# The first stretch of a token mixer, written out straight, with its rows made two chunks ahead

## The chip, the core and the metric

The kernel runs on one core of one Trainium2 chip. The metric is device time in microseconds (us), the median of several runs. The engines are TensorE (PE in the rows; PEld is its weight load), VectorE (DVE), ScalarE (ACT), GpSimd (POOL) and SyncE (SP), which here only issues DMAs.

## What is computed

```python
xn = layernorm(x)                                 # x: (4, 1024, 256), eps 1e-5, no scale or shift
out = x + attention(xn) + experts(xn)
# attention: q, k, v = xn @ W + b, 16 heads of 16, causal softmax, @ Wo + bo
# experts:   scores = softmax(xn @ gate_w.T), top 4 of 16, weights normalised
#            y = sum_e w_e * (silu(xn @ w_gate[e]) * (xn @ w_up[e])) @ w_down[e]   (width 176)
#            + a shared expert of width 352, kept as two tiles of 176
```

All is float32. The kernel keeps float32 operands as pairs of float16, a high and a low half, and multiplies high by high, high by low and low by high.

## The kernel before

The program has three blocks, between which all engines meet: `prepare`, `route`, `attention_and_experts`. The change is in `prepare` alone.

`prepare` walks through the 4096 tokens in 8 chunks of 512 rows (NCH = 8), each 4 tiles of 128 (TPC = 4). For every chunk:

- GpSimd issues the load of X (two buffers). VectorE takes the statistics (`variances`: bn_stats, bn_aggr, L445 adds eps, L447 the reciprocal), ScalarE takes the square root (`root`, L353), VectorE refines it by a Newton step of four chained four-element instructions (`newton`, L452 to L455) and normalises (`normalise`, L459, into XN).
- ScalarE makes the high half of the rows (`rows_high`, L360), VectorE the low half (`rows_low`, L465), TensorE turns both (`turn`, L540), ScalarE copies them out (`columns`, L370, into XT).
- TensorE makes q and k in four products (L554, two PSUM buffers), ScalarE copies each out twice (`product`, L386 in float32, L389 as high half), VectorE makes the low half (`low_half`, L469). Then come the router's logits (L565) and the values (L575; copied by VectorE, `values`, L477).
- Two experts' weights are split: ScalarE the high halves (`weights_high`, L377 and L378), VectorE the low halves (`weights_low`, L487 and L490). Float32 weights are staged in two buffers (gu_stage and dn_stage). GpSimd issues the three loads of an expert (`load_expert`, L281 to L283) when the low half of the tile that used the buffer before is made (semaphore `lo_made`).
- SP stores rows, columns, q, k and values to DRAM.

Each engine has its own queue of instructions, written out by hand in a function `step(c, p, first, last)`, and waits on semaphores. In step c the engines make q, k, v and logits of chunk c and the rows of chunk c + 1. ScalarE's order in a step is product 0, product 1, root and rows_high of c + 1, first expert, product 2, product 3, columns of c + 1, logits, second expert. VectorE's is variances of c + 1, low halves 0 and 1, normalise and rows_low of c + 1, first expert, low halves 2 and 3, values, second expert. `over_steps` writes steps 0, 1, 6 and 7 out and runs steps 2 to 5 as a loop of two iterations of two steps. The two shared tiles are split before step 0, experts 2c and 2c + 1 in step c.

Ahead of the steps GpSimd issues the loads of X for chunks 0 and 1 and of the two shared tiles, then fills V, woP, Vs and Ks (L301 to L305, Ks with ONES in one instruction of 6144 elements a partition) and makes identity and mask tiles (L313, L322).

Of the kernel before, what the change touches and what calls it, by code (L numbers as in the profile page):

```python
# [10 lines left out]
ALU = mybir.AluOpType  # L11
ACT = mybir.ActivationFunctionType
AX = mybir.AxisListType
P = 128
# [110 lines left out]
def wait_apart(eng, sem, value, passed):  # L125

    eng.wait_ge(sem, value)
    eng.sem_inc(passed, 1)


# [19 lines left out]
def prepare(nc, s):  # L150
# [6 lines left out]
    EPC = E // NCH  # L157
    assert EPC == SH == 2 and NCH % 2 == 0 and NCH >= 6 and s.QC == 2 and s.HG == 2 * MO
    with ExitStack() as ctx:
# [8 lines left out]
        gu = sb("gu_stage", [P, EPC, HC, 2, I])  # L168
        dn = sb("dn_stage", [IP, EPC, 2, D])
# [10 lines left out]
        rfin = sb("rfin", [P, TPC])  # L180
        F = sb("F", [P, 2, CH])
# [9 lines left out]
        sp_passed = sem("sp_passed"); dve_passed = sem("dve_passed")  # L191
        const_set = sem("const_set"); const_made = sem("const_made"); wo_clear = sem("wo_clear"); wo_in = sem("wo_in")
        gu_in = [sem(f"gu_in{i}") for i in range(EPC)]; hi_made = sem("hi_made"); lo_made = sem("lo_made")
# [4 lines left out]
        rstd_done = sem("rstd_done"); nw_done = sem("nw_done"); xn_done = sem("xn_done"); xhi = sem("xhi"); xlo = sem("xlo")  # L198
# [3 lines left out]
        xr_st = sem("xr_st"); xt_st = sem("xt_st"); qk_st = [sem(f"qk_st{i}") for i in range(4)]; v_st = sem("v_st")  # L202
# [5 lines left out]
        def over_steps(eng, step):  # L208


            for p in range(2):
                step(p, p, True, False)
            with eng.Fori(1, NCH // 2 - 1) as cc:
                for p in range(2):
                    step(cc * 2 + p, p, False, False)
            for p in range(2):
                step(NCH - 2 + p, p, False, True)

        def more(p, last):

            return not (last and p == 1)

        @block.sync
        def _(sp):
# [17 lines left out]
            def store_rows(c, p):  # L242
                wait_apart(sp, xlo, TPC * (c + 1), sp_passed)
                sp.dma_start(s.xrow_d[bass.ds(c * CH, CH), :].rearrange("(j p) d -> p j d", p=P),
                             XR[:, p].rearrange("p j a d -> p j (a d)")).then_inc(xr_st, 16)

            def step(c, p, first, last):
                wait_apart(sp, xt_done, TPC * (c + 1), sp_passed)
                sp.dma_start(s.xcol_d[bass.ds(c * TPC, TPC)].rearrange("j p f -> p j f"),
                             XT[:, p].rearrange("p j a c t -> p j (a c t)")).then_inc(xt_st, 16)  # L250
                for i in range(4):
                    dst, m = (s.q_d, s.k_d)[i // MO], i % MO
                    b = c // 2 if isinstance(c, int) else (c - p) // 2
                    wait_apart(sp, f2_done, 4 * c + i + 1, sp_passed)
                    sp.dma_start(dst[bass.ds(b, 1), :, 2 * m:2 * m + 2, :, :, :, p * CH:(p + 1) * CH]
                                 .rearrange("o a g e r j t -> (o g e r j) a t"), F2[:, i]).then_inc(qk_st[i], 16)
                    if i == 0 and more(p, last):
                        store_rows(c + 1, 1 - p)
                wait_apart(sp, v_out, 2 * HG * (c + 1), sp_passed)
                b = c // 2 if isinstance(c, int) else (c - p) // 2  # L260
                w = TPC * s.VW
                sp.dma_start(s.v_d[bass.ds(b, 1), :, :, p * w:(p + 1) * w].rearrange("o g p x -> p (o g) x"),
                             V[:, :, :].rearrange("p (g x) e -> p g (x e)", g=HG)).then_inc(v_st, 16)

            store_rows(0, 0)
            over_steps(sp, step)
            sp.wait_ge(wo_in, 16 * (4 * HG + 1))
            sp.wait_ge(xr_st, 16 * NCH)
            sp.wait_ge(xt_st, 16 * NCH)
# [5 lines left out]
        def _(pool):  # L275
            def load_x(p, src):
                pool.dma_start(X[:, p], src.rearrange("(j p) d -> p j d", p=P)).then_inc(x_in[p], 16)

            def load_expert(n, g, u, d):

                pool.dma_start(gu[:, n, :, 0, :], g.rearrange("(c p) i -> p c i", p=P)).then_inc(gu_in[n], 16)  # L281
# [3 lines left out]
            for p in range(2):  # L285
                load_x(p, s.xf[p * CH:(p + 1) * CH, :])
# [11 lines left out]
            for n in range(SH):  # L298
                c = slice(n * I, (n + 1) * I)
                load_expert(n, s.sw_gate[:, c], s.sw_up[:, c], s.sw_down[c, :])  # L300
# [4 lines left out]
            pool.memset(s.Ks[:, :, :, :], ONES).then_inc(k_ones, 1)  # L305
            pool.wait_ge(k_ones, 1)
# [17 lines left out]
            pool.wait_ge(const_made, 2)  # L324

            def step(c, p, first, last):
                if not last:

                    pool.wait_ge(xn_done, TPC * (c + 1))
                    load_x(p, s.xf[bass.ds((c + 2) * CH, CH), :])  # L330
                for n in range(EPC):
                    e = c * EPC + n
                    pool.wait_ge(lo_made, 2 * (c * EPC + n + 1))
                    load_expert(n, *(w[bass.ds(e, 1)].rearrange("o r c -> (o r) c") for w in (s.w_gate, s.w_up, s.w_down)))
# [1222 lines left out]
```

## Time and profile before

| | us |
|---|---|
| median of 3 runs | 1351.32 |
| lowest, highest | 1346.31, 1351.62 |
| the profiled execution, whole | 1356.54 |
| its span | 1354.9 |
| `prepare` in it | 0 to 142.4 |
| `route` | 142.4 to 168.9 |
| `attention_and_experts` | from 168.9 |

Over the whole span the profile has TensorE busy for 1007.9 us (74%), VectorE for 866.0 (64%), ScalarE for 654.5 (48%) and GpSimd for 579.2 (43%). All times below are us from the start of the span. An instruction's row gives its start and its duration; in brackets stand the idle time of its engine before it and what ended that. For a DMA the duration is that of its issue; the time to landing stands in the DMA view. PEclk is the share of TensorE's full clock that was granted.

### The profile page before, as it was taken

The numbers are of one execution on the slowest core, as the hardware profiler recorded it, in microseconds if no ns is written. First come the engines' busy times: TensorE is split into PE (matmuls) and PEld (weight loads), VectorE is DVE, ScalarE is ACT, GpSimd is POOL, SyncE is SP. The second block draws the span as 40 slices with busy tenths as digits, with TensorE's granted clock in tenths as the row PEclk, the third lists the DMA queues.
The fourth block names the chain that finished last, engine by engine and source line by source line (L and its number), as shares of the span: only waits on it lengthen the run. The fifth ranks groups of instructions, "written<-read, shape, count | busy, mean of one in ns | idle before, by whom it ended". The sixth has DMA issues, their size and how long they took to land.

```text
span 1354.9 us, 26394 instructions
## 1 busy us (share of the span) xinstructions
PE 1007.9 (74%) x8634; PEld 525.7 (39%) x8634; DVE 866.0 (64%) x1784; ACT 654.5 (48%) x1219; POOL 579.2 (43%) x531
## 2 busy tenths in 40 slices
PE   2788121010399999898998989998988989899885
PEld 1555010000144444444544444454444445444433
DVE  6888831000288887777777676676767676677553
ACT  3778100000154545565566666556666665566341
POOL 6333177776200000454366666435656553464100
PEclk9888555555599999899999999999989999899888
DMA  6899450010113131443545355354535353444702
GB/s 175 270 297 283 125 180 1 1 34 1 43 56 105 54 104 48 88 85 75 89 80 112 63 111 95 66 89 78 111 57 112 56 112 64 88 71 73 134 17 31
DMA packets 99484, 126.41 MB, mean 93 GB/s; under 512 B 24873, under 2 KB 83514, under 8 KB 98834
## 3 DMA queue, kind: packets, MB, share of 16 engines
q0 software_dynamic: 41632, 60.79, 25.0%
q1 hardware_dynamic: 57730, 63.99, 16.1%
q8 instruction: 77, 1.26, 0.4%
q14 instruction: 45, 0.37, 0.1%
HBM read 71.63 MB, written 57.80 MB: 96 GB/s over the span
## 4 chain that ended last, share of the span: by engine, by line
PE 53%; DVE 10%; another core or an unknown queue 10%; issue 9%; ACT 2%; SPq 1%; DMA 1%; POOL 0%; ACTq 0%; DVEq 0%
PE gup L1221 12%; PE pvp L1144 10%; PE outs L1248 9%; DVE part L1314 6%; PE smp L1100 6%; PE turn L1233 4%; PE stp L1125 4%; PE outs L1151 3%; PE turn L1191 3%; PE smp L1083 1%; ACT probs L1484 1%; DVE hf L1371 1%; DVE sg L1366 1%; DMA Qs<-nm 1%
## 5 line engine op out<-in xcount | busy, mean ns | idle before, releaser
L1484 ACT ACTIVATE probs<-stp 128x1024 f32<-128x1024 f32 (+1 forms) x320 | 300.4, 939 | 424.4 <-remote 205.2
L1314 DVE TENSOR_REDUCE part<-smp 128x2 f32<-128x256 f32 (+2 forms) x372 | 345.9, 951 | 140.0 <-remote 72.5
L942 POOL DMA_INDIRECT XG<-xrow_d,slots x144 | 146.8, 1019 | 247.0 <-DMA out<-Y 201.7
L1221 PE MATMUL gup<-gu_w,XC 128*128 (+1 forms) x1152 | 212.8, 321 | 32.7 <-issue 21.8
L1100 PE MATMUL smp<-Ks,Qs 48*128 48x128 f16 (+2 forms) x744 | 112.5, 341 | 103.7 <-DVE part L1314 52.4
L1248 PE MATMUL outs<-dn_w,h 88*128 (+1 forms) x1248 | 183.6, 280 | 0.1
L949 POOL DMA_INDIRECT out<-Y,slots x72 | 117.1, 1626 | 139.1 <-ACT Y L1517 107.8
L1144 PE MATMUL pvp<-probs,Vs 128*32 128x512 f32 (+3 forms) x1536 | 168.8, 512 | 0.8 <-DVE probs L1413 0.7
L949 POOL DMA_INDIRECT acc_d<-Y,slots x72 | 114.7, 1594 | 123.7 <-ACT Y L1517 104.6
L1221 PEld LDWEIGHTS gup<-gu_w,XC 128*128 128x128 f16 x1152 | 107.2, 99 | 96.1 <-issue 43.5
L931 POOL DMA_INDIRECT slot_d<-entry,slot_i x128 | 124.3, 971 | 41.6 <-issue 41.6
L1366 DVE SCALAR_TENSOR_TENSOR sg<-th,gup 128x176 f32<-128x176 f32 x208 | 69.8, 336 | 106.6 <-ACT th L1490 69.3
L1376 DVE TENSOR_TENSOR h<-turn,h 88x256 f16<-88x256 f32 x208 | 86.6, 416 | 78.1 <-ACT h L1496 67.2
L1248 PEld LDWEIGHTS outs<-dn_w,h 88*128 88x128 f16 x1248 | 123.3, 99 | 29.3 <-issue 2.5
L1496 ACT ACTIVATE h<-turn 88x256 f16<-88x256 f32 x208 | 78.3, 377 | 115.5 <-PE turn L1233 110.5
L1125 PE MATMUL stp<-Qs,Ks 50*128 50x512 f16 (+3 forms) x768 | 118.7, 332 | 16.2 <-DMA Qs<-nm 8.0
L1100 PEld LDWEIGHTS smp<-Ks,Qs 48*128 48x128 f16 x744 | 28.9, 94 | 199.8 <-DVE part L1314 99.8
L1233 PE MATMUL turn<-ident,hf 128*88 128x128 f32 x416 | 87.7, 294 | 22.9 <-issue 17.8
L1413 DVE TENSOR_TENSOR probs<-probs,keepk 128x512 f32<-128x512 f32 x128 | 87.7, 685 | 22.9 <-ACT probs L1484 16.3
L1490 ACT ACTIVATE th<-gup 128x176 f32<-128x176 f32 x208 | 66.4, 319 | 53.8 <-PE gup L1221 35.2
L1501 ACT ACTIVATE XC<-turn 128x512 f16<-128x512 f16 x144 | 85.3, 593 | 5.3 <-PE turn L1191 4.0
L1517 ACT ACTIVATE Y<-outs,slots 128x256 f32<-128x256 f32 x144 | 68.0, 472 | 31.9 <-PE outs L1248 27.9
(170 smaller groups left out, 1109.6 us busy)
## 6 DMA issues: line engine op xcount, KB each, us to landing
rb<-rsum_d SPq DMA_DIRECT2D x60, 128.0 KB
Ks<-k_d SPq DMA_DIRECT2D x96, 64.0 KB
Qs<-q_d SPq DMA_DIRECT2D x96, 64.0 KB
v_d<-V SPq DMA_DIRECT2D x8, 544.0 KB, 4.6
Vs<-v_d SPq DMA_DIRECT2D x16, 272.0 KB, 3.0
acc_d<-YA SPq DMA_DIRECT2D x1, 4224.0 KB
X<-L_attn_x POOLq DMA_DIRECT2D x8, 512.0 KB, 5.0
xrow_d<-XR SPq DMA_DIRECT2D x8, 512.0 KB, 5.0
```

Of the source, the lines that this page charges most:

```text
L931: pool.indirect_dma_start(s.slot_d, bass.IndirectOffsetOnAxis(ap=s.slot_i[:, i:i + 1], axis=0), s.entry[:, i, :], None).then_inc(scattered ...
L942: pool.indirect_dma_start(XG[:, q].rearrange("p a c t -> p (a c t)"), None, s.xrow_d, bass.IndirectOffsetOnAxis(ap=slots[:, r, 0:1], axis= ...
L949: pool.indirect_dma_start((s.out, s.acc_d)[r % 2], bass.IndirectOffsetOnAxis(ap=slots[:, r, 0:1], axis=0), Y[:, r % YB], None, compute_op= ...
L1100: last = pe.matmul(banks[:, e, col:col + w], Qs[rows, buf, j, t * P:(t + 1) * P], Ks[rows, buf, j, k0:k0 + w], start=i == 0, stop=k0 + w < ...
L1125: last = pe.matmul(stp[:, e, i * w:(i + 1) * w], Ks[rows, buf, j, t * P:(t + 1) * P], Qs[rows, buf, j, q * CH + q0:(q + 1) * CH], start=i ...
L1144: last = pe.matmul(pvp[32 * h:32 * h + 32, q0:CH], Vs[:, buf, o:o + 2 * DK], probs[:, st % PB, h * w:(h + 1) * w], start=t == 0, stop=t == ...
L1221: last = pe.matmul(gup[:, 0:2 * I], columns[:, a, h], weights_of(s.gu_w, e, b, h, slice(0, 2 * I)), start=n == 0, stop=n == 5)
L1233: last = pe.transpose(hp[:, c * P:(c + 1) * P], hf[:, v % FB, c * IP:(c + 1) * IP], s.ident[:, :])
L1248: last = pe.matmul(yp, h16[:, v % 2, a, c], weights_of(s.dn_w, e, b, c, slice(0, D)), start=begin and n == 0, stop=end and n == 5)
L1314: last = dve.tensor_reduce(part[:, g % 2, k0 // CH, :, j, t], banks[:, :, col:col + w], AX.X, ALU.max)
L1413: dve.tensor_tensor(block, block, s.keepk[:, :].rearrange("p (h k) -> p h k", h=1).broadcast_to([P, 4, P]), ALU.min).then_inc(masked, 1)
L1484: act.activation(to, of, ACT.Exp, scale=float(DK) ** -0.5 / QS ** 2).then_inc(exp_done, 1)
```

## The change

- `over_steps`, its loop and `wait_apart` go: all 8 steps are written out, with constant indices.
- The rows are made two chunks ahead: chunks 0 and 1 ahead of step 0, chunk 2 in step 0, chunk c + 2 in step c; the statistics of chunk c + 3 at the end of step c. The transposes and `columns` stay one chunk ahead. `rows_high` and `rows_low` of c + 2 come behind the second pair of products (step 0 has an order of its own).
- The Newton step goes from VectorE to GpSimd, ahead of the step's loads there.
- Both (or three) weight tiles of a step stand at its end, on ScalarE and VectorE. Step 0 has the two shared tiles, steps 1 to 5 have experts 0 to 9, step 6 has 10, 11 and 12, step 7 has 13, 14 and 15. The two stage buffers stay.
- Ks is filled by six instructions of 1024 elements a partition, in steps 0, 1, 6 and 7 of GpSimd's queue, instead of one ahead of the steps.
- TensorE turns chunk 0 before the gate's weights, and waits for the gate's low half only ahead of the first logits. Semaphores of the row and column stores are doubled.

The core of the diff (a short rename of indices is left out):

```diff
+        SPLITS = [[E, E + 1]] + [[2 * c - 2, 2 * c - 1] for c in range(1, NCH - 2)] + [[10, 11, 12], [13, 14, 15]]
+        ORDER = [e for step in SPLITS for e in step]
...
 @block.sync
+            def step(c):
...
+                if later(c, 2) is not None:
+                    store_rows(c + 2)
+                sp.wait_ge(v_out, 2 * HG * (c + 1))
...
 @block.gpsimd
+            def load_expert(k):
+                e, n = ORDER[k], k % 2
+                if k >= 2:
+                    pool.wait_ge(lo_made, 2 * (k - 1))
...
+            def newton(c):
+                def then(i, ins):
+                    ins.then_inc(nw_done, 1)
+                    pool.wait_ge(nw_done, 3 * c + i + 1)
+                pool.wait_ge(rstd_done, c + 1)
+                then(0, pool.tensor_tensor(nw[:, 0], rstd[:, :], rstd[:, :], ALU.mult))
+                then(1, pool.tensor_tensor(nw[:, 1], nw[:, 0], re_[:, :], ALU.mult))
+                then(2, pool.tensor_scalar(nw[:, 2], nw[:, 1], -0.5 / (XS * XS), 1.5, ALU.mult, ALU.add))
+                if c:
+                    pool.wait_ge(xn_done, TPC * c)
+                pool.tensor_tensor(rfin[:, :], rstd[:, :], nw[:, 2], ALU.mult).then_inc(rfin_done, 1)
...
+            newton(0)
             pool.memset(V[:, :, DK:DK + 1], 1.0).then_inc(v_ones, 1)
...
-            pool.memset(s.Ks[:, :, :, :], ONES).then_inc(k_ones, 1)
...
+            load_x(2)
+            newton(1)
+            load_x(3)
+            newton(2)
+
+            def step(c):
+                if later(c, 2) is not None and c:
+                    newton(c + 2)
+                if c < 2 or c >= NCH - 2:
+                    for b in range(c % 2, NB, 2):
+                        pool.memset(s.Ks[:, b, 0 if c < 2 else 1], ONES).then_inc(k_ones, 1)
+                if c:
+                    first = sum(len(x) for x in SPLITS[:c])
+                    for k in range(first, first + len(SPLITS[c])):
+                        load_expert(k)
+                if c + 4 < NCH:
+                    load_x(c + 4)
...
 @block.scalar
+            def step(c):
                 product(c, 0)
+                if c and later(c, 2) is not None:
+                    root(c + 2)
                 product(c, 1)
-                if more(p, last):
-                    root(c + 1)
-                    rows_high(c + 1, 1 - p)
-                weights_high(c, 0)
+                if c == 0:
+                    rows_high(1)
+                    act.wait_ge(gt_out, 1)
+                    act.activation(g16[:, 0], gT32[:, :, :], ACT.Copy, scale=WS).then_inc(w_hi, 1)
                 product(c, 2)
                 product(c, 3)
-                if more(p, last):
-                    columns(c + 1, 1 - p)
+                if c == 0:
+                    root(2)
+                elif later(c, 2) is not None:
+                    rows_high(c + 2)
                 act.wait_ge(lg_done, c + 1)
...
+                if later(c, 1) is not None:
+                    columns(c + 1)
+                if c == 0:
+                    rows_high(2)
+                first = sum(len(x) for x in SPLITS[:c])
+                for k in range(first, first + len(SPLITS[c])):
+                    weights_high(k)
...
 @block.vector
+            def step(c):
                 low_half(c, 0)
                 low_half(c, 1)
+                if c and later(c, 2) is not None:
+                    normalise(c + 2)
+                if c == 0:
+                    rows_low(1)
+                    variances(2)
+                    dve.wait_ge(w_hi, 4)
+                    dve.scalar_tensor_tensor(out=g16[:, 1], in0=gT32[:, :, :], scalar=WS, in1=g16[:, 0],
+                                             op0=ALU.mult, op1=ALU.subtract).then_inc(w_lo, 1)
                 low_half(c, 2)
                 low_half(c, 3)
+                if c == 0:
+                    normalise(2)
+                elif later(c, 2) is not None:
+                    rows_low(c + 2)
                 values(c, 0)
                 values(c, 1)
+                if c == 0:
+                    rows_low(2)
+                if later(c, 3) is not None:
+                    variances(c + 3)
+                first = sum(len(x) for x in SPLITS[:c])
+                for k in range(first, first + len(SPLITS[c])):
+                    weights_low(k)
+
+            variances(0)
+            normalise(0)
+            variances(1)
+            rows_low(0)
...
 @block.tensor
+            pe.wait_ge(const_made, 1)
+            turn(0)
             pe.wait_ge(b_in, 16 * (2 * HG + 2))
...
+            pe.wait_ge(w_lo, 3)
+            for c in range(NCH):
+                step(c)
```

`later(c, n)` is c + n, or None where there is no such chunk.

## Rows read from the trace of the kernel before

**Rows 1.** Busy time by stretch: PE, PEld, DVE, ACT, POOL, then PEclk, DMA share, GB/s
```profile
69.87:85.59 15.72, 12.44 (x98) 7.89 (x97) 12.80 (x38) 11.95 (x24) 5.11 (x7) 0.78 0.96 306
85.59:100.10 14.51, 11.28 (x98) 6.92 (x96) 12.76 (x38) 9.82 (x21) 5.11 (x7) 0.88 0.86 264
...
114.37:128.24 13.87, 11.06 (x98) 7.04 (x97) 12.51 (x38) 10.84 (x24) 4.44 (x7) 0.88 0.89 272
128.24:142.40 14.16, 8.95 (x81) 5.24 (x80) 9.66 (x22) 8.70 (x16) 2.18 (x3) 0.90 0.89 295
...
168.90:360.00 191.10, 21.03 (x155) 8.81 (x155) 24.52 (x31) 1.34 (x2) 134.01 (x142) 0.50 0.16 44
```

**Rows 2.** TensorE in order of time: the first products of chunks 0, 1, 7
```profile
25.60 7.84 PE L554 MATMUL qk<-XT,w 128*128 128x512 f16 x24 [1.39 <-ACT XT L370]
...
41.37 5.58 PE L554 MATMUL qk<-XT,w 128*128 128x512 f16 x24
...
128.24 5.59 PE L554 MATMUL qk<-XT,w 128*128 128x512 f16 x24
```

**Rows 3.** Waits until 143 us: total, number, longest
```profile
PE tp L540 <- DVE XR L465: 25.9, 8, 6.6
```

**Rows 4.** ScalarE in order of time: copies of a product, high halves of experts
```profile
66.52 0.67 ACT L386 ACTIVATE F<-qk,bqk 128x512 f32<-128x512 f32 x1
67.09 0.68 ACT L389 ACTIVATE F<-qk,bqk 128x512 f16<-128x512 f32 x1
...
78.58 0.78 ACT L377 ACTIVATE gu_w<-gu_stage 128x704 f32 x1
79.26 0.62 ACT L378 ACTIVATE dn_w<-dn_stage 88x512 f32 x1
...
138.27 0.79 ACT L377 ACTIVATE gu_w<-gu_stage 128x704 f16<-128x704 f32 x1 [2.35 <-DMA dn_stage<-L_ffn_w_down]
```

**Rows 5.** VectorE in order of time: ahead of chunk 0, and the refining of chunk 3
```profile
10.02 5.85 DVE L445 TENSOR_SCALAR re_<-mv 128x4 f32<-128x4 f32 x1
...
17.54 1.65 DVE L459 TENSOR_SCALAR XN<-X,mv,rfin 128x256 f32<-128x256 f32 x4
...
19.21 1.28 DVE L514 TENSOR_TENSOR w<-F,w 128x512 f16<-128x512 f32 x2
...
21.84 1.43 DVE L465 TENSOR_TENSOR XR<-XN,XR 128x256 f16<-128x256 f32 x4 [0.56 <-ACT XR L360]
...
28.98 1.39 DVE L438 BATCH_NORM_STATS2 st<-X 128x6 f32<-128x256 f32 x4
...
30.73 0.17 DVE L445 TENSOR_SCALAR re_<-mv 128x4 f32<-128x4 f32 x1
...
61.50 0.15 DVE L452 TENSOR_TENSOR nw<-rstd 128x4 f32<-128x4 f32 x1
...
62.09 0.16 DVE L455 TENSOR_TENSOR rfin<-rstd,nw 128x4 f32<-128x4 f32 x1
```

**Rows 6.** GpSimd in order of time: before the steps, and the first of an expert's issues
```profile
8.66 0.77 POOL L283 DMA_DIRECT2D dn_stage<-L_ffn_sw_down  x1
...
10.61 5.23 POOL L305 MEMSET Ks<- 128x6144 f16 x1
15.99 0.95 POOL L313 TENSOR_SCALAR_AFFINE_SELECT idh<-idh 64x256 bf16<-64x256 bf16 x2
...
67.44 0.71 POOL L281 DMA_DIRECT2D gu_stage<-L_ffn_w_gate  x1 [2.19 <-DVE dn_w L490]
```

**Rows 7.** DMA view, three stretches: GB/s by slice; issues, KB, median us to landing
```profile
GB/s 357 363 353 218 192 176 376 398 360 345 232 43 335 373 354 363 315 152 212 364 327 356 299 276 82 204 380 366 376 302 224 181 220 354 351 254 271 181 246 303
...
dn_stage<-L_ffn_w_down POOLq DMA_DIRECT2D x16, 176.0 KB, 5.6
...
dn_stage<-L_ffn_w_down POOLq DMA_DIRECT2D x2, 176.0 KB, 4.2
...
dn_stage<-L_ffn_sw_down POOLq DMA_DIRECT2D x2, 176.0 KB, 7.0
```

More of the change, by code:

```diff
@@ L206, in flat, with one, expert_parts, later @@
             return w.rearrange("p c n -> p (c n)")
[L208 to L221, printed above, removed]
+        def one(t):
+            return t.rearrange("p o c n -> p (o c) n")
+        def expert_parts(e):
+            e = slice(e, e + 1) if isinstance(e, int) else bass.ds(e, 1)
+            return ([one(s.gu_w[:, e, a]).rearrange("p c (a i) -> p c a i", a=2) for a in range(2)],
+                    [one(s.dn_w[:, e, a]) for a in range(2)])
+        SPLITS = [[E, E + 1]] + [[2 * c - 2, 2 * c - 1] for c in range(1, NCH - 2)] + [[10, 11, 12], [13, 14, 15]]
+        ORDER = [e for step in SPLITS for e in step]
+        assert sorted(ORDER) == list(range(E + SH))
+        def later(c, ahead):
+            return c + ahead if c + ahead < NCH else None
         @block.sync
@@ L297, in _ @@
             last.then_inc(const_made, 1)
[L298 to L300 removed]
+            for k in range(SH):
+                load_expert(k)
+            newton(0)
             pool.memset(V[:, :, DK:DK + 1], 1.0).then_inc(v_ones, 1)
@@ L324, in _ @@
             pool.wait_ge(const_made, 2)
[L326 to L334, printed above, removed]
-            over_steps(pool, step)
-            pool.wait_ge(k_ones, 1)
-        def one(t):
-            return t.rearrange("p o c n -> p (o c) n")
-        def expert_parts(c, n):
-            e = slice(E + n, E + n + 1) if c is None else bass.ds(c * EPC + n, 1)
-            return ([one(s.gu_w[:, e, a]).rearrange("p c (a i) -> p c a i", a=2) for a in range(2)],
-                    [one(s.dn_w[:, e, a]) for a in range(2)])
+            load_x(2)
[11 more added lines that the diff above has]
+                    for k in range(first, first + len(SPLITS[c])):
+                        load_expert(k)
+                if c + 4 < NCH:
+                    load_x(c + 4)
+            for c in range(NCH):
+                step(c)
+            pool.wait_ge(k_ones, 2 * NB)
         @block.scalar
@@ L557, in step @@
                     x.then_inc(qk_done, 1)
-                if more(p, last):
-                    turn(c + 1, 1 - p)
-                if began:
+                if later(c, 1) is not None:
+                    turn(c + 1)
+                if c:
                     pe.wait_ge(lg_out, c)
+                else:
+                    pe.wait_ge(w_lo, 4)
                 for j in range(TPC):
@@ L584, in _ @@
             last.then_inc(gt_done, 1)
-            turn(0, 0)
-            pe.wait_ge(w_lo, 4)
-            over_steps(pe, step)
+            pe.wait_ge(w_lo, 3)
+            for c in range(NCH):
+                step(c)
 def route(nc, s):
```

204 lines of the change are left out of this document (88 added, 116 removed).

## Prediction

> **What bounds the kernel now.** I read the stretch by stretch table first. The change touches only the first stretch, up to 142.40 us; behind it come routing and 191 us in which TensorE is nearly idle and GpSimd busy, then attention with the experts [rows 1]. All engines leave the first stretch together, so a microsecond won or lost before 142.40 moves everything behind it by as much, and nothing later gets shorter. Next, TensorE's timeline: chunk 0 begins at 25.60, chunk 1 at 41.37, chunk 7 at 128.24 [rows 2]. Chunks 1 to 6 take (128.24 - 41.37) / 6 = 14.5 us each; chunk 7 with the end of the stretch takes 14.2. In a chunk TensorE works some 11.1 us and else stands mostly at the transposes of the next rows, 25.9 us in eight waits [rows 1, 3]: these rows are normalised, split and turned within the chunk, VectorE and ScalarE in turns. VectorE works 12.5 to 12.8 us a chunk, ScalarE 9.8 to 12, and the DMA share is 0.86 to 0.96 [rows 1]. No compute in the middle waits for an expert's load: one whose three issues start at 67.44 is first read at 78.58; only the last expert is waited for, 2.35 us [rows 4, 6].
>
> **The start.** VectorE's four-element add at L445 takes 5.85 us in chunk 0 and 0.17 in chunk 1, and it ends as GpSimd's 5.23 us fill of Ks ends [rows 5, 6]. That fill is cut into six slices and spread. The add then ends near 10.2, the reciprocal at 10.4, the root at 10.6. The refining of the root is now GpSimd's, behind its first loads, the last of which is issued at 8.66 [rows 6]. Its price N no row shows. Lower bound: on VectorE the four chained steps take 0.8 us [rows 5]. Upper bound: two chained selects of GpSimd take 0.95, so four 1.9 [rows 6], and some 2.5 if VectorE's operations hold them up; the held add is no bound, since it was held by a fill of 6144 elements. I take N = 1.3, nearer to the lower row, as these have four elements a partition: 11.9. GpSimd then fills V, woP and Vs, 1.4 us, and normalising is of the kind that was held at L445: 13.3. Then VectorE in its new order: normalising 1.6, statistics of chunk 1 2.0, low halves of the rows 1.3, low halves of the weights 1.9, to 20.1 [rows 5]. TensorE turns and ScalarE copies chunk 0 beside it, so chunk 0 starts at 20.3 for 25.60. **Gain 5.3.** The gate's transposes hide behind chunk 0's turn.
>
> The Trainium skill (GPSIMD Engine Reference, Key points) says that GpSimd shares its SBUF interfaces with VectorE and that VectorE is about twice as fast for elementwise work. By it the refining would be some 1.6 us instead of 0.8, and each round of the loop below 0.3 longer. The held add of 5.85 us agrees with the sharing [rows 5].
>
> **Chunk 0.** From its start: rows of chunk 1 low at 8.4, then VectorE makes chunk 2's statistics (2.1) and the gate's low half (0.2), on which the logits now wait, 10.7; logits 0.9, values 3.3: 14.9, for 15.77 now. So chunk 1 starts at 35.2 for 41.37. By then VectorE is behind: values to 36.0, low rows of chunk 2 37.4, statistics of chunk 3 39.4, root 39.6, refining 40.9, a Ks slice (5.23 / 6 = 0.87) 41.8. Only now come the loads of step 1: five issues ahead of the last at 0.71 to 0.77 each (3.6 us), the last one's landing, and its high half. The landing is 5.6 us as the median of sixteen, 4.2 at the light end, 7.0 for six issues on end at the start [rows 6, 7]; I take 5.5. 41.8 + 3.6 + 5.5 + 1.2 = 52.1. I call this moment H(1): ScalarE done with step 1's second expert.
>
> **The loop that then sets the pace.** Before, an expert's load waits for its stage alone. Now the refining stands on GpSimd's queue ahead of six issues; its root stands on ScalarE behind product(c,0), and that behind the high halves of the step before. From H to H: product(c,0), two activations at a pitch of 0.57, 1.1; root and hand-over 0.3; N 1.3; five issues 3.6; landing 5.5; high halves of gu and dn 1.3 [rows 4, 6, 7]. **13.1 us.** VectorE's own work is 12.5 in a straight chunk less 0.8 of refining, 11.7; TensorE's 11.1 [rows 1, 5]. The traffic is 512 KB each for X, xrow and xcol, four times 256 for q and k, 544 for v and six times 176 for experts, 4.26 MB; at the 340 to 390 GB/s of the full slices it takes 10.9 to 12.5 [rows 7]. All lie under 13.1. So H(5) = 52.1 + 4 x 13.1 = 104.5: 1.4 us a chunk less than now.
>
> **The tail, where most of it goes back.** Steps 6 and 7 make three experts each, with two stages. The third load of a step waits for the low half of the step's first expert, which VectorE makes behind the step's values. Counted from H(5): qk of chunk 6 to 4.0, turn, logits and values on TensorE 5.4: 9.4, and chunk 7 may start, at 113.9, 14 us ahead of now. VectorE's values 10.3, low half of expert 10 11.7, expert 12's load 1.4 to its last issue and 5.2 to land, 18.3, high half 19.6 = H(6). ScalarE stands at it, and the products of chunk 7 are queued behind; TensorE makes two of them and idles some 8 us. Then two copies of products 22.0, the last qk 23.5, logits and values 27.3, VectorE 28.2, low half of expert 13 29.6, and only then expert 15's load: 1.4 + 5.0, 36.0; its high and low halves 38.1; all leave at 38.2. The stretch ends at 104.5 + 38.2 = **142.7** for 142.40. From where chunk 7 may start it is 28.8 us, for 14.2 now [rows 1, 4].
>
> **Edges at nothing.** Straight code: chunk 6, straight now, takes 13.9, those of the loop up to 15.7, so straight code isn't starved, and what it saves is off the loop above [rows 1]. SP's row store goes behind four product stores, and chunk 0's column store behind the rows of chunk 1; their readers come a chunk later, and what they cost is what is missing to that. X is loaded behind the experts and read 10 us later. The 17 loads of wo begin 3 us later on SP and are wanted at the end. The late Ks slices run while GpSimd waits for stages.
>
> **The sum.** The profiled execution is 1354.9 in span and 1356.54 in all, 5.2 over the median of 1351.32. The change is +0.3: 1356.8, or 1351.6 on the median. I say **1352**, since a schedule made by hand forgets waits oftener than it invents them.
>
> **Rivals.** *Forecast*, 1345 to 1358: start and pace gain 14 us and the tail gives them back. 0.62.
> *Loads land sooner.* With the light landing of 4.2 and N at 0.8 the loop is 11.3, and VectorE's 11.7 decides: H(5) = 50.3 + 46.8 = 97.1, the tail 2 shorter, the end 133.3: 9 us gained, 1342. For it: steps 6 and 7 load no X and store no rows. Against: 5.6 is the median now, and the same bytes will come closer together. If the tail moreover takes 14 us as now, 1337. Together 0.20. The Trainium skill (DMA: Bandwidth & Descriptors, Anatomy of one DMA) gives about 2.0 us and bytes over 436 GB/s for a GpSimd DMA, as an estimate 2.4 for 176 KB; the loop would be 10.0, and VectorE's 11.7 would decide as well. The rows of 4.2 to 7.0 speak against it under this traffic [rows 7].
> *The queue of loads takes the place of the wait removed: slower.* 4.26 MB in 13.1 us is 325 GB/s, for 264 to 306 now [rows 1]. With a landing of 6.5 and N 2.1 the loop is 14.9: H(5) = 53.9 + 59.6 = 113.5, the tail 2 longer, the end 153.7: 1362. Landing and N together decide: slower than before from 6.8 on (6.8 is what I take), by over 0.5% from about 8.1. For it: the 7.0 at the start; against: the issues alone take 4.4 us of each loop and leave the queue gaps. 0.18.
> *Rows two chunks ahead bring nothing*, since ScalarE's queue holds them: the time of the forecast, which has that in its loop.
>
> **Numbers.** A measurement can tell about 0.5%, 6.8 us. Faster 0.20, same 0.62, slower 0.18. The 80% range takes in most of both rivals, 1342 to 1360.
>
> **What would show it.** Right: L445's first instance at 0.2 us and the first product at 20 to 21; chunk starts 13 us apart from chunk 2 on; ScalarE waiting for dn_stage's landing in each step; TensorE idle for 8 us within chunk 7; a last expert load issued near 134, the routing's first reduction at 142 to 144. Wrong: chunks under 12 us apart or ScalarE never waiting for a load, a routing start before 137; or refining operations of over 0.6 us each, or landings over 6.5.

## The result, and the profile after

The changed kernel is slower: 1368.8 us as the median of six runs (1364.8 to 1372.5) against 1351.5 of the kernel before in the same six rounds (1346.3 to 1357.3), a ratio of 1.0123 with an interval of 1.0093 to 1.0154. Forecast was 1352, with a range up to 1360. The profiled execution took 1367.0 in span and 1368.74 in all, for 1354.9 and 1356.54 before. The first stretch now ends where routing's first reduction starts. Behind that point the two profiles are alike: 1354.9 - 142.5 = 1212.4 before, 1367.0 - 155.8 = 1211.2 after. The loss lies in the first stretch and is 13.3 us there.

```profile
155.81 0.69 DVE L723 TENSOR_REDUCE mx<-logits 128x32 f32<-128x512 f32 x1 [0.33 <-PEq L152]
```

TensorE in order of time, the pairs of products of the changed kernel, to be held against [rows 2]. "x12" is one pair; in brackets the idle time before it.

```profile
20.25 8.11 PE L579 MATMUL qk<-XT,w 128*128 128x512 f16 x24 [1.07 <-ACT XT L388]
36.16 2.75 PE L579 MATMUL qk<-XT,w 128*128 128x512 f16 x12
...
49.90 2.76 PE L579 MATMUL qk<-XT,w 128*128 128x512 f16 x12 [2.02 <-ACT XT L388]
57.86 5.30 PE L579 MATMUL qk<-XT,w 128*128 128x512 f16 x12 [5.20 <-ACT F L405]
67.80 2.76 PE L579 MATMUL qk<-XT,w 128*128 128x512 f16 x12 [0.27 <-ACT XT L388]
72.27 2.76 PE L579 MATMUL qk<-XT,w 128*128 128x512 f16 x12 [1.70 <-ACT F L405]
...
116.80 4.91 PE L579 MATMUL qk<-XT,w 128*128 128x512 f16 x12 [5.55 <-ACT F L405]
...
125.86 2.75 PE L579 MATMUL qk<-XT,w 128*128 128x512 f16 x12
137.10 5.00 PE L579 MATMUL qk<-XT,w 128*128 128x512 f16 x12 [8.48 <-ACT F L405]
```

The 5.4 us of the start are there: chunk 0 begins at 20.25 for 25.60, chunk 1 at 36.16 for 41.37. By chunk 7 most is gone, 125.86 for 128.24. From there the stretch takes 29.9 us for 14.3. The eight waits for the transposes' rows [rows 3] have become one, ahead of chunk 0; in the middle TensorE now waits for ScalarE to copy a product out ("ACT F").

The windows of the changed kernel, with the columns of [rows 1], are cut at the chunk starts:

```profile
36.16:49.90 13.74, 10.01 (x99) 6.14 (x96) 13.67 (x43) 10.61 (x22) 9.31 (x13) 1.00 0.81 255
49.90:67.80 17.90, 12.43 (x96) 6.93 (x97) 11.76 (x34) 10.88 (x23) 7.04 (x12) 0.81 0.92 271
67.80:79.70 11.90, 9.84 (x97) 6.20 (x97) 11.17 (x33) 10.52 (x22) 7.00 (x11) 1.00 0.93 298
79.70:96.20 16.50, 11.44 (x96) 6.62 (x97) 12.65 (x38) 10.88 (x23) 6.70 (x11) 0.90 0.96 299
...
125.86:155.70 29.84, 11.18 (x82) 5.87 (x79) 14.01 (x28) 12.06 (x21) 9.77 (x13) 0.71 0.53 163
```

Chunk 1 is filled by VectorE (13.67 of 13.74). Chunks 2 to 6 last about 12 and 17 us in turns, 15.2 on average, and no engine is busy for that long: in the three shown VectorE has 11.2 to 12.7, ScalarE 10.5 to 10.9. So a chain with waits sets the pace. The last window is the tail, where VectorE and ScalarE together have 26 us of work in 29.8, no more than if they worked in turns. The waits of the changed kernel up to 156 us (total, number, longest) name the links:

```profile
POOL nw L300 <- ACT rstd L372: 44.9, 8, 9.2
...
PE qk L579 <- ACT F L405: 29.5, 8, 8.5
ACT gu_w L394 <- DMA dn_stage<-L_ffn_w_down: 28.5, 10, 7.3
POOL gu_stage L289 <- DVE dn_w L506: 25.9, 5, 9.5
```

ScalarE waits for the landing of an expert's third load ten times, 28.5 us in all. Before it did so once, for 2.35 [rows 4]. GpSimd waits for the root eight times; in five of them, in steps 1 to 5, the step's loads are queued behind that wait. TensorE waits for ScalarE, which stands at the weights. That is a ring: root, refining, loads, landing, high halves, next root. One round of it, from GpSimd's and then ScalarE's timeline in step 1:

```profile
40.97 0.51 POOL L300 TENSOR_TENSOR nw<-rstd 128x4 f32<-128x4 f32 x1 [4.18 <-ACT rstd L372]
41.56 1.35 POOL L301 TENSOR_TENSOR nw<-nw,re_ 128x4 f32<-128x4 f32 x1
42.99 0.51 POOL L302 TENSOR_SCALAR nw<-nw 128x4 f32<-128x4 f32 x1
43.58 0.52 POOL L305 TENSOR_TENSOR rfin<-rstd,nw 128x4 f32<-128x4 f32 x1
...
48.62 0.77 POOL L291 DMA_DIRECT2D dn_stage<-L_ffn_w_down  x1
```

```profile
55.35 0.79 ACT L394 ACTIVATE gu_w<-gu_stage 128x704 f16<-128x704 f32 x1 [3.29 <-DMA dn_stage<-L_ffn_w_down]
56.04 0.61 ACT L395 ACTIVATE dn_w<-dn_stage 88x512 f16<-88x512 f32 x1
```

The four refining steps take 3.1 us here, from 40.97 to 44.10. The last load is issued at 48.62 and ScalarE's high half starts at 55.35, 6.7 us later. H(1), the moment at which ScalarE is done with step 1's second expert, is 56.6. The same reading gives H at 71.0, 86.0, 99.9 and 115.6 for steps 2 to 5, one round every 14.7 us. Below, H is always the start of the last L395 (or what that line has become) of a step plus 0.6.

### The profile page after: what moved, and what is told of

It reads as the page before. It is cut to its first block, busy times and chain, and to the rows that moved or that the text cites. A ratio compares the mean times of both kernels' runs of the same rounds, so it can differ in the third digit from the quotient of the medians.

```text
span 1367.0 us, 25847 instructions
## 1 busy us (share of the span) xinstructions
PE 1005.0 (74%) x8634; PEld 520.2 (38%) x8634; DVE 855.5 (63%) x1752; ACT 654.6 (48%) x1220; POOL 596.0 (44%) x568
## 3 DMA queue, kind: packets, MB, share of 16 engines
q1 hardware_dynamic: 57730, 63.99, 16.2%
## 4 chain that ended last, share of the span: by engine, by line
PE 49%; another core or an unknown queue 14%; DVE 9%; issue 8%; DMA 2%; SPq 2%; ACT 2%; POOL 0%; ACTq 0%; DVEq 0%
PE gup L1249 11%; PE pvp L1172 9%; PE outs L1276 8%; PE smp L1128 5%; DVE part L1342 5%; PE turn L1261 4%; PE stp L1153 4%; PE outs L1179 3%; PE turn L1219 2%; DMA Qs<-nm 1%; PE smp L1111 1%; ACT probs L1512 1%; DVE sg L1394 1%; DVE hf L1399 1%
## 5 line engine op out<-in xcount | busy, mean ns | idle before, releaser
L1276 PEld LDWEIGHTS outs<-dn_w,h 88*128 88x128 f16 x1248 | 122.6, 99 | 29.8 <-issue 4.0
```

What stands on the lines that cost most here:

```text
L1276: last = pe.matmul(yp, h16[:, v % 2, a, c], weights_of(s.dn_w, e, b, c, slice(0, D)), start=begin and n == 0, stop=end and n == 5)
```

## The experiments

**Three theories.** R: the ring sets the pace, and the refining's place ahead of the loads is what makes it. S: there are too few stages (two buffers for two or three experts), so that loads start late wherever the refining stands. V: VectorE's order or the straight code costs the time. Eleven kernels were run. The end of the stretch is read in each trace at the same instruction, routing's first reduction; ratios are against the kernel before on the same chip.

| kernel | end of stretch | median us | ratio (interval) |
|---|---|---|---|
| before | 142.5 | 1351.5 | |
| after | 155.8 | 1368.8 | 1.0123 (1.0093 to 1.0154) |
| e1: refining on VectorE | 142.6 | 1353.2 | 1.0027 (0.9988 to 1.0066) |
| e2: four stages | 139.9 | 1352.2 | 0.9988 (0.9956 to 1.0020) |
| e3: four stages, loads a step ahead | 124.7 | 1338.2 | 0.9883 (0.9811 to 0.9954) |
| e4: before, with the fill of Ks cut | 141.9 | 1349.9 | 0.9979 (0.9946 to 1.0012) |
| e5: refining behind the loads | 154.7 | 1366.2 | 1.0107 (1.0049 to 1.0165) |
| e6: e1 and e2 | 128.2 | 1338.0 | 0.9912 (0.9881 to 0.9944) |
| e7: e1 and e3 | 127.0 | 1336.1 | 0.9898 (0.9865 to 0.9930) |
| e8: e3, step 1's experts earlier still | 125.2 | 1334.4 | 0.9882 (0.9846 to 0.9919) |
| e9: two experts in every step | 142.6 | 1358.2 | 1.0041 (1.0016 to 1.0066) |
| e10: refining twice | 155.8 | 1373.0 | 1.0177 (1.0133 to 1.0220) |
| e11: e1 and e9 | 130.3 | 1344.1 | 0.9925 (0.9885 to 0.9966) |

### The ring: e1, e5, e10

**e1** takes the refining off GpSimd's queue and leaves the rest of the change.

```diff
 def normalise(c):
-    dve.wait_ge(rfin_done, c + 1)
+    dve.wait_ge(rstd_done, c + 1)
+    then(c, 0, dve.tensor_tensor(nw[:, 0], rstd[:, :], rstd[:, :], ALU.mult))
+    ... (the other three steps)
@@ gpsimd step
-    newton(c + 2)
```

> The changed kernel with one edit: the four refining steps of the root are VectorE's again, ahead of the normalising, and no longer stand on GpSimd's queue ahead of the expert loads. Theory A (the loop product, root, refining, six issues, landing, high half sets the pace, 14.7 us a step in the changed kernel): the loads of a step start 3 to 4 us sooner, and then VectorE's own 12.5 us of work decide. From step 1 to step 5 the interval between the ends of the second high halves falls from 14.7 to 12.4 to 13.0; the stretch ends 8 to 11 us sooner, near 146, and the time is about 1360. Theory B (the DMA traffic sets the pace, the loads only land when the stores let them): the interval stays at 14 or more and the time within 4 us of the changed kernel's 1368.8.

The stretch ends 13.2 us earlier than after, at 142.63, and the slowdown is gone. H is 51.5, 63.6, 76.2, 88.7 and 103.2; chunks 2 to 5 start 12.57 us apart. A window of e1 over one such chunk:

```profile
60.88:73.45 12.57, 9.84 (x96) 6.18 (x96) 12.36 (x39) 10.58 (x23) 5.09 (x7) 1.00 1.04 345
```

VectorE has 12.36 us of work in 12.57: it is the bound, with 0.8 of refining on it. R holds, V falls. More came back than expected, because H(1) comes 5.2 earlier and four rounds take 12.9 on average for 14.7; the tail gives 0.8. H(5) = 103.2 and a tail of 39.4 are also near the forecast's 104.5 and 38.2, but by another road: VectorE's work sets the round, not the ring of 13.1.

Three of the four rounds are 12.2 to 12.6 us and the last is 14.5. In the chunk of the last one, 86.02 to 100.89, VectorE is busy for 14.66 us, 2.3 more, and the normalising, 1.66 us a step earlier, takes 2.72. It stands beside two of GpSimd's Ks slices (95.36, 1.86 us):

```profile
95.61 2.72 DVE L465 TENSOR_SCALAR XN<-X,mv,rfin 128x256 f32<-128x256 f32 x4
```

It takes 2.73 in e6 and e11, beside the same two. The forecast put the late slices at nothing; in the changed kernel they fall beside no normalising, but once the ring is gone the chunk with two of them is some 2.3 us longer.

**e5** leaves the refining on GpSimd and puts it behind the step's loads.

```diff
 def step(c):          # gpsimd
-    if later(c, 2) is not None and c:
-        newton(c + 2)
...
     load_expert(k)    # two or three
+    if later(c, 2) is not None and c:
+        newton(c + 2)
```

> The changed kernel with one edit: on GpSimd's queue the refining of the root stands behind the step's expert loads instead of ahead of them. It tells the place in the queue from the price of the refining itself. Theory A (each queue is walked in order): the loads start sooner, so ScalarE's waits for a landing shrink; but the normalising on VectorE, which stands ahead of low halves 2 and 3 and of everything behind them, now waits for six issues, 4.4 us; VectorE's round is then 12.5 + 3 to 4 us. Interval 15 to 16.5 us a step, time 1372 to 1380, slower than the changed kernel. Theory C (the loads' late start alone is what costs): interval 13, time near 1358.

Expected was a time above that of after. The median is 2.6 us under it, and the intervals of the two overlap. H(1) comes at 54.0, 2.7 earlier; then three rounds take 14.67 each and the fourth 16.2, no shorter than after's. The ring is another one. The waits of e5 up to 156 us:

```profile
DVE XN L476 <- POOL rfin L305: 18.0, 7, 3.3
```

and GpSimd's timeline in one step:

```profile
71.59 0.72 POOL L289 DMA_DIRECT2D gu_stage<-L_ffn_w_gate  x1 [6.71 <-DVE dn_w L506]
...
75.17 0.79 POOL L291 DMA_DIRECT2D dn_stage<-L_ffn_w_down  x1
75.95 0.24 POOL L300 TENSOR_TENSOR nw<-rstd 128x4 f32<-128x4 f32 x1
76.27 0.20 POOL L301 TENSOR_TENSOR nw<-nw,re_ 128x4 f32<-128x4 f32 x1
76.56 0.18 POOL L302 TENSOR_SCALAR nw<-nw 128x4 f32<-128x4 f32 x1
76.83 0.20 POOL L305 TENSOR_TENSOR rfin<-rstd,nw 128x4 f32<-128x4 f32 x1
```

The low half of a step's first expert frees the first stage at 71.6, six issues take 4.4 us, the refining 1.1. Then VectorE, which had stood still for 3.2 us, normalises (77.07), and its low half of the next step's first expert frees that stage at 86.3, one round of 14.7 later. It waits once a step for what GpSimd does behind six issues. The trouble is a refining that shares a queue with the refills of its own step, ahead of them or behind: both orders close a ring through VectorE's or ScalarE's next step.

**e10** does the first three refining operations twice in every step.

```diff
-then(0, ...); then(1, ...); then(2, ...)
+for again in range(2):
+    then(3 * again, ...); then(3 * again + 1, ...); then(3 * again + 2, ...)
```

> A dose: the changed kernel with the first three refining steps on GpSimd made twice, same results. The three cost 1.3 to 2.9 us a step in the changed kernel's trace. Theory A: they lie on the loop, so each step from 1 to 5 gets longer by what they take, 1.2 to 2 us, and chunk 0's start later by 0.9: stretch end 7 to 11 us later than 155.8, time about 1377. If the refining were off the loop: within 3 us of 1368.8.

This missed. The stretch ends at 155.80, where it did in after, for 7 to 11 us later expected, and the median moved by 4 us for 8. The groups of GpSimd's operations in steps 1 to 5, of e10 from 36 to 115 us first, and then of after from 36 to 110 us (busy total, mean ns, idle before):

```profile
L302 POOL TENSOR_TENSOR nw<-rstd 128x4 f32<-128x4 f32 x10 | 5.8, 583 | 33.7 <-ACT rstd L374 33.3
```

```profile
L300 POOL TENSOR_TENSOR nw<-rstd 128x4 f32<-128x4 f32 x5 | 3.6, 729 | 33.9 <-ACT rstd L372 33.9
L301 POOL TENSOR_TENSOR nw<-nw,re_ 128x4 f32<-128x4 f32 x5 | 3.6, 719 | 0.4
```

Seven operations take 2.7 us a step in e10 (steps 2 to 5), four take 2.2 in after. In each of these steps of e10 two of the seven take 0.60 and end as an operation of VectorE does, and five in VectorE's gaps take 0.2:

```profile
59.78 0.69 DVE L488 TENSOR_TENSOR F<-F 128x512 f16<-128x512 f32 x1 [0.18 <-ACT F L407]
59.92 0.60 POOL L302 TENSOR_TENSOR nw<-rstd 128x4 f32<-128x4 f32 x1 [7.05 <-ACT rstd L374]
60.61 0.20 POOL L303 TENSOR_TENSOR nw<-nw,re_ 128x4 f32<-128x4 f32 x1
```

So more than half of the price of refining in the loop is a hold, not a price for each operation, and doubling the work does not double it. The refining grew by 0.5 us a step, the landings of the second expert came 0.4 sooner (5.8 on average), and the round grew by 0.2, to 14.9. H(5) is then 118.2, 2.6 later than in after, and the tail gives that back, so that the two stretches end at the same moment by luck. In after the second pair of chunk 6's products followed 5.55 us of idle time and took 4.91 (116.80, above). In e10, where the step began with less idle time, it took 2.76:

```profile
119.40 2.76 PE L581 MATMUL qk<-XT,w 128*128 128x512 f16 x12 [1.60 <-ACT F L407]
```

The expectation had taken the time of three operations once more for three more of them, and so counted the holds twice. This dose was too small to tell whether the refining is on the ring: the run does not speak for R, which rests on e1, e3 and the links read above.

### The tail: e2, e9, e11

**e2** has four stages for two, all else as after.

```diff
-gu = sb("gu_stage", [P, SH, HC, 2, I])
+gu = sb("gu_stage", [P, NS, HC, 2, I])       # NS = 4
...
-e, n = ORDER[k], k % 2
-if k >= 2:
-    pool.wait_ge(lo_made, 2 * (k - 1))
+e, n = ORDER[k], k % NS
+if k >= NS:
+    pool.wait_ge(lo_made, 2 * (k - NS + 1))
```

> The changed kernel with four stage buffers for expert weights instead of two, and all issues where they are. Theory A: the loop of steps 1 to 5 keeps its pace (14.7 us), since a load still stands behind the refining; but the third load of steps 6 and 7 no longer waits for the low half of the step's first expert, so the tail from the end of step 5's high halves falls from 40.2 to about 28 us and the stretch ends near 143.5: 12 us less, about 1357. Theory B (traffic): the tail falls by under 5 us, 1364 or more.

The loop did not move at all: H(5) = 114.4, a round of 14.7. So S is wrong for the loop, since with free stages the loads still stood behind the refining. The tail fell from 40.2 to 25.5 us, more than the 12 expected: with three experts in steps 6 and 7 and two stages, it had paid a load, a high half and a low half one after another, twice.

**e9** keeps two stages and gives every step two experts, the shared tiles standing ahead of step 0 as in the kernel before.

```diff
-SPLITS = [[E, E + 1]] + [[2 * c - 2, 2 * c - 1] for c in range(1, NCH - 2)] + [[10, 11, 12], [13, 14, 15]]
-ORDER = [e for step in SPLITS for e in step]
+SPLITS = [[2 * c, 2 * c + 1] for c in range(NCH)]
+ORDER = [E, E + 1] + [e for step in SPLITS for e in step]
```

> The changed kernel with the weights dealt out as in the kernel before: the two shared tiles ahead of step 0, two experts in each of steps 0 to 7, still all at the end of a step, two stages, refining on GpSimd ahead of the loads. Theory A: the pace of the loop stays at 14 to 15 us a step and now holds for steps 0 to 5; the tail is a normal step or less, about 14 us behind the start of chunk 7, with no load behind a low half of its own step. The stretch ends at 138 to 144, time about 1352. Theory B (traffic makes the tail): no gain, 1365.

The stretch ends at 142.63: the 13 us are back by this alone, and the forecast of the stretch was right. ScalarE still waits ten times for a landing, 19.9 us in all, and the rounds of steps 2 to 5 are 14.3, 13.8, 14.9 and 14.8. The median of 1358.2 is higher than the trace of this kernel explains; its interval lies a little above 1.

**e11** joins e1 and e9: no buffer is added.

> The even dealing of the first run of these together with the refining on VectorE; two stages, so no more memory than the change. Theory A: steps at VectorE's 12.6 us, tail about 15: the stretch ends at 125 to 130, time 1336 to 1340, level with the versions with four stages.

1344.1 and a stretch of 130.3, a little short of what was expected. 12.2 us of stretch are gained on the kernel before with the same memory. The two edits nearly add up: 13.2 us each on after, 25.5 together. Either fault of the change alone was enough to hide its gain.

### Where the gain lay: e3, e6, e7, e8

**e3** is e2 with GpSimd issuing the experts of step c + 1 in step c; the refining stays ahead of them.

```diff
-if c:
-    first = sum(len(x) for x in SPLITS[:c])
-    for k in range(first, first + len(SPLITS[c])):
+if c + 1 < NCH:
+    first = sum(len(x) for x in SPLITS[:c + 1])
+    for k in range(first, first + len(SPLITS[c + 1])):
         load_expert(k)
```

> Four stages as in the run before it, and the loads of a step's experts issued one step earlier on GpSimd's queue (step 1's in step 0), still behind the refining there. Theory A: no high half waits for a landing any more and the loop is cut; VectorE's 12.5 us of work or TensorE's 11 set the pace, 12 to 13 us a chunk; the stretch ends near 130 and the time is about 1343, which is 8 us under the kernel before. Theory B (traffic): chunks stay at 14 or more, 1355 or more.

```profile
48.35:59.93 11.58, 9.84 (x97) 6.20 (x97) 10.85 (x31) 10.48 (x23) 7.90 (x12) 1.00 1.06 360
59.93:72.33 12.40, 9.84 (x96) 6.19 (x96) 12.29 (x39) 10.46 (x23) 8.58 (x12) 1.00 1.06 364
```

```profile
124.66 0.69 DVE L724 TENSOR_REDUCE mx<-logits 128x32 f32<-128x512 f32 x1 [1.88 <-PEq L152]
```

This is 5 us better than expected. The ring is cut at its longest link: the landing (5.7 to 6.9 us for the second experts whose loads are issued in steps 1 to 5, not shorter) is read a step later. Chunks come 12.0 us apart, with VectorE busy for 0.94 to 0.99 of a chunk, a DMA share of 1.06 and 360 to 364 GB/s in the two shown. VectorE and the DMA engines are both near their end, and no run tells for certain which decides; e7 below, with 0.8 of work more on VectorE and the same traffic, has chunks 0.6 longer, which speaks for VectorE. TensorE's clock is full in these windows. No run gives the kernel before these stages and early loads, so how much of the 12.0 for 14.5 is owed to the rows made ahead is open.

**e6** (e1 and e2) and **e7** (e1 and e3) ask if the refining's place still matters once the loads have room.

> Both earlier edits together: the refining on VectorE and four stage buffers, loads in the step that uses them. Theory A: steps 1 to 5 at the 12.6 us that the run with the refining on VectorE had, and the tail at the 26 us that the run with four stages had: the stretch ends near 130, time about 1340. If the two gains are the same gain twice, it ends at 138 or later, 1348.

> The run with four stages and loads one step ahead, with the refining on VectorE. Theory A: there the refining is on no loop with the loads any more, and 12.0 us a chunk is near the DMA rate (331 GB/s in the mean over 44 to 125 us, slices of 375 to 380), so its place hardly matters: within 4 us of that run's 1338. Rival D: GpSimd's refining, 2.4 to 3.2 us a step there, was still what held VectorE and set the 12.0; the time falls by 5 us or more.

Both came out as expected: 1338.0 and 1336.1. e7's chunks are 12.57 apart, again VectorE's work with its 0.8 of refining, for 12.0 with the refining on GpSimd. So the move to GpSimd is worth 0.6 us a chunk in the traces, near the forecast's "12.5 less 0.8", but only where the step's own loads don't wait behind it; the medians of e3 and e7, 1338.2 and 1336.1, do not show it.

**e8** loads step 1's experts ahead of step 0 as well.

```diff
 load_x(3)
+for k in range(SH, SH + len(SPLITS[1])):
+    load_expert(k)
 newton(2)
```

> The run with four stages and loads one step ahead, with step 1's two experts loaded ahead of step 0 as well. If the DMA rate sets the pace from chunk 1 on, 1.08 MB moved out of it into a stretch where the queues are half empty gives back up to 2.9 us: about 1335.5. If the engines set it, no change: 1338.

It has the lowest median, 1334.4, and is not told apart from e3; its stretch is not shorter (125.2), so the added edit shows no gain in the trace. Either beats both given kernels, by 1.2% and 2.4%, at the price of two more stage buffers.

### The start: e4

**e4** is the kernel before with the fill of Ks cut into six.

```diff
-pool.memset(s.Ks[:, :, :, :], ONES).then_inc(k_ones, 1)
...
 def step(c, p, first, last):       # gpsimd
+    if first or last:
+        for b in range(p, NB, 2):
+            pool.memset(s.Ks[:, b, 0 if first else 1], ONES).then_inc(k_ones, 1)
```

> The kernel before with one edit: the 6144-element fill of Ks ahead of the steps is cut into six slices placed in steps 0, 1, 6 and 7 of GpSimd's queue, as in the change. Theory A: VectorE's first four-element add at L445 falls from 5.85 to about 0.2 us, chunk 0's first product starts at 20 to 21 instead of 25.6, and all of it is kept to the end: 5 us less than the kernel before, about 1346.5. Rival: what the start gains is lost at a later wait (bvb's load at 15.4 us, or the stages), and the time is within 2 us of 1351.5.

Chunk 0 starts at 22.43, for 25.60 before and 20 to 21 expected, but the stretch ends at 141.91 for 142.50, and the time is the same: the rival of the expectation came true. VectorE's add, with the fill of woP that stays ahead of the steps, and one of its refining operations in chunk 5, with two late slices of Ks:

```profile
9.48 0.99 POOL L302 MEMSET woP<- 128x1024 f32 x1
9.83 0.86 DVE L446 TENSOR_SCALAR re_<-mv 128x4 f32<-128x4 f32 x1
```

```profile
102.08 1.86 POOL L327 MEMSET Ks<- 128x1024 f16 x2
103.11 0.86 DVE L455 TENSOR_SCALAR nw<-nw 128x4 f32<-128x4 f32 x1
```

Of the 5.85 us of [rows 5] 5.0 were the fill of Ks; the fills of woP and Vs still hold the add until 10.69. They stand behind the refining in the changed kernel, where the add takes 0.17, and e4 keeps the old order of VectorE too; it gets 3.2 of the 5.3 us.

This lead is not worn away slowly. Chunks 1 to 5 start 3.1 to 3.4 us ahead of the kernel before, chunk 6 starts 1.4 ahead and chunk 7 0.7. It is lost in the chunks in which the late slices stand. In chunk 5, the longest of the run (16.2 us for 14.3), two slices run, the refining operation above takes 0.86 for 0.17, and the products of the values behind it take 4.39 for 3.10, at a granted clock of 0.61 for 0.88. That the hold brought on the longer products is argued from their order. The chunk's later loads wait for VectorE (109.05), not for the slices. So a microsecond won at the start is kept through the middle here, and is lost where the slices went.

## Why the prediction was wrong, point by point

**The step that failed.** It is the sum of the loop: two of its terms were too small. The refining on GpSimd, N, was put at 1.3 us and took 2.2 on average; the landing of a step's last load was put at 5.5 and took 6.2. The round was 14.7 us instead of 13.1, and both terms stand once more in H(1), where they took 3.1 and 6.7. Together they make 9.4 of the 13.1 us by which the end of the stretch was missed. With 13.1 the pace would have gained 1.4 us a chunk and paid for the tail; with 14.7 it gained nothing on the 14.5 of the kernel before. That the ring sets the pace, and that the tail gives back what is won, was right. The points in order:

**Where the stretch ends and what that is worth: right in the trace.** Behind the stretch the profiled pair agrees to 1.2 us (the medians differ by more, see below), and the sum had to be made there. Forecast end 142.7, measured 155.8.

**The start: right.** L445's successor takes 0.17 for 5.85 and chunk 0 starts at 20.25 for a forecast of 20.3:

```profile
9.89 0.17 DVE L467 TENSOR_SCALAR re_<-mv 128x4 f32<-128x4 f32 x1
...
11.68 2.80 DVE L476 TENSOR_SCALAR XN<-X,mv,rfin 128x256 f32<-128x256 f32 x4 [1.41 <-POOL rfin L305]
```

The parts moved within it. Refining took 1.0, from 10.60 to 11.64, as VectorE stood idle. Normalising was held by the fills piece by piece and took 2.80, where 1.4 of hold and 1.6 of work were put one after the other.

**Chunk 0 and H(1): 4.5 us short.** The refining of step 1 starts at 40.97, not 39.6 (1.4). Up to its root VectorE runs without a gap from the normalising of chunk 2 on, which took 2.85 us, for 1.4 undisturbed. Two Ks slices ran beside it (32.76, 1.84 us); the forecast had counted their time on GpSimd, and no hold of VectorE:

```profile
32.86 2.85 DVE L476 TENSOR_SCALAR XN<-X,mv,rfin 128x256 f32<-128x256 f32 x4 [0.66 <-POOL rfin L305]
```

The refining took 3.1, not 1.3 (1.8). The last load took 6.7 to land, not 5.5 (1.2). The rest is 0.1. H(1) is 56.6, not 52.1. Chunk 1's start, 36.16 for 35.2, is not on this path.

**The loop: the mechanism right, two terms mis-sized.** From H to the refining 1.34 on average (1.4 said). Refining, to the end of its last operation, 1.85, 2.68, 1.85 and 2.40, mean 2.2 (N = 1.3 said). Issues 3.7 (3.6). Landing 6.3, 5.8, 5.7 and 6.9, mean 6.2 (5.5). High halves 1.3 (1.3). That makes 14.7 for 13.1, and four rounds of it 6.6 us. N was bounded by 0.8 and 2.5, and the value was chosen by the size of the operations, nearer the lower row. The rows that bore on it were of another kind: GpSimd is held while VectorE runs, as VectorE had been held at L445 [rows 5], and in the loop the refining falls where VectorE is at work. Alone the four operations take 1.0 (start) and 1.1 (e5); in steps 1 to 5 of the changed kernel 1.85 to 3.1. For the landing, the median over all loads was taken where the term was that of the sixth issue on end. The forecast read [rows 7]'s 7.0 as that of six issues on end; it is the median of the two shared tiles' loads, 6.7 for the third issue and 7.4 for the sixth. In steps 1 to 4 the second experts' landings were indeed the longer ones (5.7 to 6.7, the first experts' 4.1 to 4.7). The forecast had named both as signs of being wrong: refining operations of over 0.6 us (the first two took 0.73 and 0.72 on average) and landings over 6.5 (6.7 and 6.9 in steps 1 and 5).

**The tail: the mechanism right, 2 us short.** From H(5) to the end 40.2 for 38.2. TensorE idles for 8.48 us within chunk 7, said 8. What was not in the sum is TensorE's clock behind idle time. H(6) came 20.3 behind H(5), said 19.6, with the pair at 116.80 on the path in 4.91 for 2.76. The pair at 137.10 ran at a granted clock of 0.54 and took 5.00, so chunk 7's last products were done 26.5 behind H(5), said 23.5. The terms behind them, said 14.7, came out at 13.7, which leaves 2.0:

```profile
137.10:142.10 5.00, 5.00 (x19) 1.89 (x20) 2.05 (x3) 2.36 (x4) 2.22 (x3) 0.54 0.61 153
```

ScalarE's two long waits in the tail are the two serial loads; the last one's issues are at 148.14 to 149.59, where 134 was said:

```profile
134.59 0.79 ACT L394 ACTIVATE gu_w<-gu_stage 128x704 f16<-128x704 f32 x1 [6.61 <-DMA dn_stage<-L_ffn_w_down]
...
153.16 0.79 ACT L394 ACTIVATE gu_w<-gu_stage 128x704 f16<-128x704 f32 x1 [7.26 <-DMA dn_stage<-L_ffn_w_down]
```

**The sum of the misses.** 4.5 + 6.6 + 2.0 = 13.1, and 155.8 - 142.7 is 13.1.

**The rivals.** What happened is the third, the queue of loads that takes the place of the wait removed, and to the slower side: landing 6.2 (6.5 said), N 2.2 (2.1), a round of 14.7 (14.9), H(5) = 115.6 (113.5), end 155.8 (153.7). It was given 0.18. It has the forecast's mechanism and differs from it in the two sizes that failed. The held add and the 6.7 to 7.4 us of loads issued in a burst, the rows nearest in kind, spoke for the rival's. The range ended at 1360, under that rival's own 1362, although a size that recurs in each round carries its error as often. *Loads land sooner* did not occur. The Trainium skill (DMA: Bandwidth & Descriptors, Anatomy of one DMA) gives, as an estimate from its figures, 2.4 us for such a load; each landing of steps 1 to 5 took 4.1 to 6.9. *Rows two chunks ahead bring nothing* is not settled: in e3 they come with chunks of 12.0 for 14.5, but with four stages and early loads as well.

**What stays open.** The profiled pair differs by 12.1 us, and the stretch by 13.3, while the medians differ by 17.3. 13.3 us is 1.0% and within the interval, but no run shows where the other 4 would be. Span less end of stretch varies from 1204.7 to 1216.6 over the traces of all kernels, which have the same code there. The edge prices put at nothing (straight code, stores, wo) weren't tested one by one; e1 and e6, which have all of them, end 3.4 and 1.8 us before the ends expected of them, which leaves no room for a large one. The Ks slices were counted too low, by 1.4 us in H(1) and, in e1 and e6, by some 2.3 us late in the stretch.

## What to carry to other kernels

When an operation moves to another queue, walk the ring it joins there, all the way to its own next instance: a step's small work on the queue that refills the buffers of that step puts issue, landing and conversion between one round and the next, ahead of the refills or behind them. Take the refills out of the ring first, by issuing them a step ahead with buffers to spare, and move the small work then; and check the last steps, where more tiles than buffers in one step make load, high half and low half serial. A fill moved out of the way at the start is not gone: look at what stands beside it where it now runs. In a sum, a term of the ring counts once a round: take its value from rows of the same kind and place in a burst, not from a median over all, and let the range carry the rounds.

## What the runs showed of the hardware

**GpSimd's tiny operations beside VectorE.** A four-element operation takes 0.18 to 0.24 us while VectorE stands still (e5, and 10.60 in after) and up to 1.35 in after while it runs; in e3 one took 2.13:

```profile
10.60 0.19 POOL L300 TENSOR_TENSOR nw<-rstd 128x4 f32<-128x4 f32 x1 [1.28 <-ACT rstd L372]
```

```profile
51.99 2.13 POOL L301 TENSOR_TENSOR nw<-rstd 128x4 f32<-128x4 f32 x1 [3.37 <-ACT rstd L373]
```

The Trainium skill (GPSIMD Engine Reference, Key points) says that the two engines share their SBUF interfaces, and the traces agree in kind: 0.2 us alone and up to 2.13 beside VectorE. By its factor of two for elementwise work the refining would be, as an estimate, 1.6 us; it was 1.0 alone and 1.85 to 3.1 in steps 1 to 5.

**A product behind idle time.** In the changed kernel a pair of products that followed 1.7 to 2.1 us of idle time took 2.76; pairs that followed 4.7 to 8.5 us of it took 4.4 to 5.3, at a granted clock of 0.50 to 0.63 over the pair, which is the lower of the two levels, 1.2 GHz, for most of it (2.4 GHz is the other). The two kinds in windows of after:

```profile
57.86:63.20 5.34, 5.34 (x15) 2.04 (x16) 3.55 (x7) 2.45 (x6) 4.95 (x9) 0.50 0.69 215
72.27:75.00 2.73, 2.73 (x15) 1.29 (x16) 2.18 (x4) 2.25 (x5) 2.34 (x4) 1.00 0.95 330
```

In steps 1 to 5 the lower clock cost little, as ScalarE still came to wait for a landing at their end; in the tail it was on the path twice.
